# Second feed-forward: gelu twice on ScalarE, four gelu buffers, the convolution taps' wide operations on GpSimd

## What is computed

```python
h = jnp.einsum('bsd,dh->bsh', x, W_exp) + b_exp
h = butterfly(h, up_weights, D_HIDDEN)
h = jax.nn.gelu(h + up_bias, approximate=False)
h = butterfly(h, down_weights, D_HIDDEN)
y = jnp.einsum('bsh,hd->bsd', h, W_con) + b_con
return y + down_bias
```

```python
dt = jnp.exp(log_dt)[:, None]
A = -jnp.exp(log_A_real) + 1j * A_imag
dtA = A * dt
C = (C_real + 1j * C_imag) * (jnp.exp(dtA) - 1.0) / A
vand = jnp.exp(dtA[:, :, None] * t)
K = 2.0 * jnp.einsum('dn,dnl->dl', C, vand).real
```

## Time and profile before

| | us |
|---|---|
| median of 3 runs (2667.52 to 2676.39) | 2668.12 |
| the profiled execution | 2671.26 |
| its span, first to last instruction | 2669.2 |
| TensorE matmuls busy in it | 2289.9 (86%) |
| VectorE busy | 1659.8 (62%) |
| ScalarE busy | 1372.6 (51%) |
| GpSimd busy | 1200.8 (45%) |

### The profile page before, as it was taken

One profiled execution on the slowest core, in us unless ns is written; L12 is line 12 of the kernel. 1 busy time (PEld: TensorE's weight loads), 2 busy tenths in 40 slices (PEclk: granted clock), 3 DMA queues, 4 the chain that ended last, 5 costly groups with the idle time before them and its releaser, 6 DMA issues. The chain is left out here.

```text
span 2669.2 us, 55063 instructions
## 1 busy us (share of the span) xinstructions
PE 2289.9 (86%) x20336; PEld 1601.9 (60%) x20336; DVE 1659.8 (62%) x4170; ACT 1372.6 (51%) x2116; POOL 1200.8 (45%) x1245
## 2 busy tenths in 40 slices
PE   7957777777999888988889987889899879999979
PEld 4535555555666555555555554778566756666658
DVE  6757778776113477767767764666444447777753
ACT  4522222222332288877887885442311457777653
POOL 4329999991001177656756752122365003223220
PEclk9979999998999899999999999999999989999999
DMA  5554445541000111111111111000000100000001
GB/s 179 151 173 135 141 142 153 160 136 63 17 1 28 40 57 56 63 52 57 49 56 53 59 51 42 8 1 1 1 0 1 38 0 1 1 1 1 1 1 64
DMA packets 158733, 149.00 MB, mean 56 GB/s; under 512 B 21441, under 2 KB 141377, under 8 KB 155393
## 3 DMA queue, kind: packets, MB, share of 16 engines
q1 hardware_dynamic: 138704, 105.51, 13.2%
q0 software_dynamic: 3456, 23.07, 2.5%
q10 hardware_dynamic: 16304, 16.83, 2.1%
HBM read 100.51 MB, written 40.63 MB: 53 GB/s over the span
## 5 line engine op out<-in xcount | busy, mean ns | idle before, releaser
L1838 POOL TENSOR_SCALAR a_dist<-a_dist,a_mq 128x512 f32<-128x512 f32 x512 | 357.1, 719 | 120.9 <-ACT a_mq L1777 120.9
L1881 DVE TENSOR_SCALAR_CACHE_REDUCE a_dist<-a_ring 128x512 f32<-128x512 f32 x512 | 332.1, 687 | 90.0 <-PE a_ring L1526 88.6
L1767 ACT ACTIVATE a_pT<-a_psT 128x1024 f32<-128x1024 f32 x256 | 258.3, 1025 | 95.4 <-PE a_psT L1538 87.7
L1538 PE MATMUL a_psT<-ident,a_dist 128*128 128x128 f32 x2048 | 266.3, 277 | 18.0 <-ACT a_pT L1767 17.8
L1538 PEld LDWEIGHTS a_psT<-ident,a_dist 128*128 128x128 f32 x2048 | 235.0, 142 | 50.2 <-issue 20.4
L1761 ACT ACTIVATE a_dist<-a_dist 128x2048 f32<-128x2048 f32 x128 | 236.9, 1902 | 45.1 <-DVE a_dist L1881 42.1
L1526 PE MATMUL a_ring<-a_stack 102*128 102x512 bf16 x512 | 184.2, 398 | 59.1 <-DVE a_dist L1881 35.1
L1526 PEld LDWEIGHTS a_ring<-a_stack 102*128 102x128 bf16 x512 | 47.6, 98 | 230.1 <-DVE a_dist L1881 165.3
L3359 ACT ACTIVATE ds_wtm<-ds_wg,ds_par 128x256 f32<-128x256 f32 x64 | 29.1, 502 | 268.2 <-DVE ds_wg L3489 264.0
L1551 PE MATMUL a_psO<-a_pT,a_va 128*32 128x512 f32 x1024 | 138.0, 616 | 2.3 <-ACT a_pT L1767 2.3
L517 POOL CAST f_h_hi<-f_h 128x512 fp32r<-128x512 f32 x64 | 46.4, 727 | 202.8 <-ACT f_h L506 202.8
(11 more groups left out here) (432 smaller groups left out, 5845.2 us busy)
## 6 DMA issues: line engine op xcount, KB each, us to landing
a_stack<-a_parts_dram SPq DMA_DIRECT2D x384, 64.0 KB
a_parts_dram<-a_parts SPq DMA_DIRECT2D x32, 384.0 KB, 2.5
bf_w<-in_up_w_dram POOLq DMA_DIRECT2D x10, 1024.0 KB
bf_w<-in_down_w_dram POOLq DMA_DIRECT2D x10, 1024.0 KB
ds_nbg<-tok_nbk ACTq DMA_DIRECT2D x128, 64.0 KB
feat_v<-di_part SPq DMA_DIRECT2D x16, 256.0 KB, 2.6
tok_nbk<-di_nbk SPq DMA_DIRECT2D x16, 256.0 KB, 3.0
feat_k<-di_part SPq DMA_DIRECT2D x16, 256.0 KB, 3.4
```

The costliest lines, as they stand in the source:

```text
L1538: last = turn(psT[:, u % 2, kb, q * P:(q + 1) * P], dist[:, g % 2, i, q, k * P:(k + 1) * P], core.ident[:])
L1767: a(pT[:, u // 2, u % 2], psT[:, u % 2], ACT.Exp).then_inc(exp_done, 1)
L1838: last = nc.gpsimd.tensor_scalar(d, d, -1.0, mq[:, g % 2, i, q:q + 1], ALU.mult, ALU.add)
L1881: ts(dist[:, gg % 2, i, q, :], ps[:], 1e-12, 3.0e38, ALU.max, ALU.min, accum_out=mq[:, gg % 2, i, q:q + 1]).then_inc(ring_out, 1)
```

## The change

Four things are edited.

- `h` gets four buffers; the gelu of group n waits for `h_lo` of group n-4.
- ScalarE runs gelu twice on the same PSUM bank: exact into `h`, then into the float32r tensor `h_hi`. GpSimd's copy goes away, and VectorE's subtraction waits for the second gelu. The four normalisations of the next batch come one each after groups 1 to 4.
- The taps' two-input operations on 1024 and 2048 elements, the negation and the eight channel masks go from VectorE to GpSimd (new method `ConvTaps.gpsimd`, 25 steps in one chain with waits for VectorE's and ScalarE's parts). VectorE keeps the 64-wide steps and two roundings. Its pieces move: `between(b, 0)` now stands ahead of a batch's first `h_lo`; the pieces run in (1,0), (1,1), (3,1) and (4,0). ScalarE's two pieces come one batch later.
- `lc_inv`, `lc_w` and `lc_b` are allocated at the other end of SBUF and loaded in `conv_spectra`'s block; their readers wait for them.

The diff, cut to its core:

```diff
+    RING = 4
-        self.h = core.sbuf(f"{tag}_h", [P, 2, S], ctx)
+        self.h = core.sbuf(f"{tag}_h", [P, self.RING, S], ctx)
...
                 act.wait_ge(self.h_ps, n + 1)
-                if n >= 2:
-                    act.wait_ge(self.h_lo_done, n - 1)
-                nc.scalar.activation(self.h[:, m % 2, :], psH[m % 2], ACT.Gelu,
+                if n >= self.RING:
+                    act.wait_ge(self.h_lo_done, n - self.RING + 1)
+                nc.scalar.activation(self.h[:, n % self.RING, :], psH[m % 2], ACT.Gelu, bias=self.bf.bias_h[:, m:m + 1])
+                if m == 0 and b:
+                    act.wait_ge(self.y_ps, TPB * b)
+                nc.scalar.activation(self.h_hi[:, m, :], psH[m % 2], ACT.Gelu,
                                      bias=self.bf.bias_h[:, m:m + 1]).then_inc(self.h_done, 1)
-                if m == NH // 2 and b + 1 < B:
-                    normalize(b + 1)
+                if b + 1 < B and m in (1, 2, 3, 4):
+                    normalize(b + 1, m - 1)
...
-    def gpsimd(self, pool):
-        for n in range(B * self.NH):
-            pool.wait_ge(self.h_done, n + 1)
-            self.nc.gpsimd.tensor_copy(self.h_hi[:, n % self.NH, :], self.h[:, n % 2, :]).then_inc(self.h_hi_done, 1)
...
-        def rest_of_hidden(b, m):
-
-            dve.wait_ge(self.h_hi_done, NH * b + m + 1)
-            tt(self.h_lo[:, m, :], self.h[:, m % 2, :], self.h_hi[:, m, :], ALU.subtract).then_inc(self.h_lo_done, 1)
+        def parts_of_hidden(b, m):
+
+            n = NH * b + m
+            dve.wait_ge(self.h_done, n + 1)
+            tt(self.h_lo[:, m, :], self.h[:, n % self.RING, :], self.h_hi[:, m, :],
+               ALU.subtract).then_inc(self.h_lo_done, 1)
...
         for b in range(B):
+            between(b, 0)
             for m in range(NH):
-                rest_of_hidden(b, m)
-                if m == NH // 2 - 1:
-                    between(b, 0)
+                parts_of_hidden(b, m)
...
         def _(pool):
-            ffn.gpsimd(pool)
+            beside.gpsimd(nc, pool)
...
+    def load_forward(self, sp):
+        sp.dma_start(self.fwd[:], self.sources[0].rearrange("(k p) n -> p k n", p=P)).then_inc(self.fwd_in, 16)
...
-    PHASES, TAPS = 14, 56
+    STEPS, WHOLE, MODES = 6, 8, 31
+    RAW, PHASES, SPREAD, TAPS = 3, 6, 17, 25
...
         if m == 0:
-            pe.wait_ge(self.vec, self.TAPS)
+            pe.wait_ge(self.wide, self.TAPS)
...
-        if n == 2:
-            act.wait_ge(self.vec, self.PHASES)
+        if n == 3:
+            act.wait_ge(self.vec, self.WHOLE)
+            act.wait_ge(self.wide, self.PHASES)
...
-        if n == 3:
+        if n == 4:
...
+        if (n, half) == (1, 1):
+            dve.wait_ge(self.wide, self.RAW)
             step(ts(f[:, 1, :], f[:, 0, :], ROUND, -ROUND, ALU.add, ALU.add))
...
-        if (n, half) == (2, 0):
+        if (n, half) == (3, 1):
             dve.wait_ge(self.act_n, self.ROOTS)
...
-        if (n, half) == (2, 1):
-            cmul_re(T0, NRE, NIM, AR, ABS, RN, FR)
-            cmul_im(T1, NRE, NIM, AR, ABS, RN, FR)
+        if (n, half) == (4, 0):
+            cmul(T0, T1, NRE, NIM, AR, ABS, RN, FR)
...
+    def gpsimd(self, nc, pool):
...
+        def step(ins):
+
+            self.wides += 1
+            ins.then_inc(self.wide, 1)
+            pool.wait_ge(self.wide, self.wides)
+
+        pool.wait_ge(self.loaded, 48)
+        pool.wait_ge(self.vec, self.STEPS)
+        step(tt(f3[0], over_i(TURN), ix, ALU.mult))
+        step(tt(g_im[:], over_j(TURN), jx, ALU.mult))
+        step(tt(self.g_mag, over_j(DR), jx, ALU.mult))
+        pool.wait_ge(self.vec, self.WHOLE)
+        step(tt(f[:, 0, :], f[:, 0, :], f[:, 1, :], ALU.subtract))
+        step(tt(f3[1], over_i(DR), ix, ALU.mult))
+        step(tt(g_im[:], g_im[:], g_re[:], ALU.subtract))
+        assert self.wides == self.PHASES
+        pool.wait_ge(self.act_n, self.ROOTS)
+        step(tt(f[:, 2, :], f[:, 2, :], f[:, 1, :], ALU.mult))
+        step(tt(f[:, 3, :], f[:, 3, :], f[:, 1, :], ALU.mult))
+        pool.wait_ge(self.act_n, self.POWERS)
+        step(tt(g_im[:], g_im[:], self.g_mag, ALU.mult))
+        step(tt(g_re[:], g_re[:], self.g_mag, ALU.mult))
+        pool.wait_ge(self.vec, self.MODES)
+        step(tt(f3[0], over_i(NRE), f3[3], ALU.mult))
+        step(tt(f3[1], over_i(NIM), f3[2], ALU.mult))
+        step(tt(self.f_re[:], f3[0], f3[1], ALU.subtract))
+        step(tt(f3[0], over_i(NRE), f3[2], ALU.mult))
+        step(tt(f3[1], over_i(NIM), f3[3], ALU.mult))
+        step(tt(self.f_im[:], f3[0], f3[1], ALU.add))
+        step(ts(self.f_im[:], self.f_im[:], -1.0, None, ALU.mult))
+        assert self.wides == self.SPREAD
+        for q in range(2):
+            for c in range(CPT):
                 dst = self.fm[:, q].rearrange("p t (i c) -> p t i c", c=CPT)[:, :, :, c]
                 step(ts(dst, (self.f_re, self.f_im)[q][:], self.chan[:, c:c + 1], None, ALU.mult))
...
+        @block.sync
+        def _(sp):
+            lc.load(sp)
+
         @block.tensor
         def _(pe):
-            pe.wait_ge(lc.loaded, 64)
+            pe.wait_ge(lc.fwd_in, 16)
...
+                if i == 0 and u == 0:
+                    pe.wait_ge(lc.loaded, 48)
...
+                            pool.wait_ge(lc.loaded, 48)
```

More of the change, by code:

```diff
@@ L479, in scalar, with normalize @@
         nc, core, psT, psH, NH = self.nc, self.core, self.psT, self.psH, self.NH
-        def normalize(b):
-            if b:
+        def normalize(b, j):
+            if b and j == 0:
                 act.wait_ge(self.tr_done, KD * b)
-            for j in range(TPB):
-                t = TPB * b + j
-                nc.scalar.activation(self.xn[:, j, :], core.X[:, t, :], ACT.Identity, bias=core.shift[:, t:t + 1],
-                                     scale=core.rstd[:, t:t + 1]).then_inc(self.xn_done, 1)
+            t = TPB * b + j
+            nc.scalar.activation(self.xn[:, j, :], core.X[:, t, :], ACT.Identity, bias=core.shift[:, t:t + 1],
+                                 scale=core.rstd[:, t:t + 1]).then_inc(self.xn_done, 1)
         def take_turned(b):
@@ L496, in take_turned @@
                 nc.scalar.activation(self.x_hi[:, k, :], psT[k], ACT.Identity).then_inc(self.x_hi_done, 1)
-        normalize(0)
+        for j in range(TPB):
+            normalize(0, j)
         take_turned(0)
@@ L903, in __init__ @@
         self.vec = core.sem("ck_vec")
+        self.wide = core.sem("ck_wide")
         self.act_n = core.sem("ck_act")
@@ L908, in __init__ @@
         self.steps = 0
+        self.wides = 0
     def allocate(self, core, ctx):
@@ L977, in vector @@
         tt, ts, stt = nc.vector.tensor_tensor, nc.vector.tensor_scalar, nc.vector.scalar_tensor_tensor
-        over_i = lambda t: spread(t, [P, NMT, NI], 2)
-        over_j = lambda t: spread(t, [P, NMT, NJ], 2)
-        f3 = [f[:, q, :].rearrange("p (t i) -> p t i", i=NI) for q in range(4)]
         def step(ins):
@@ L1049, in vector @@
-        if n in (5, 6):
-            q = n - 5
-            for c in range(half * CPT // 2, (half + 1) * CPT // 2):
+            assert self.steps == self.MODES
+    def gpsimd(self, nc, pool):
+        v, idx, f, g_re, g_im = self.v, self.idx, self.f, self.g_re, self.g_im
+        DR, TURN, NRE, NIM = (v[:, q, :] for q in (self.DR, self.TURN, self.NRE, self.NIM))
+        tt, ts = nc.gpsimd.tensor_tensor, nc.gpsimd.tensor_scalar
+        over_i = lambda t: spread(t, [P, NMT, NI], 2)
+        over_j = lambda t: spread(t, [P, NMT, NJ], 2)
+        f3 = [f[:, q, :].rearrange("p (t i) -> p t i", i=NI) for q in range(4)]
+        ix = spread(idx[:, NJ:], [P, NMT, NI], 1)
+        jx = spread(idx[:, 0:NJ], [P, NMT, NJ], 1)
+        def step(ins):
[29 more added lines that the diff above has]
+            for c in range(CPT):
```

54 lines of the change are left out of this document (15 added, 39 removed).

## The result

The changed kernel takes 2663.89 us (median of 20 runs, 2653.31 to 2675.65) beside 2673.73 for the kernel before (20 runs, 2666.5 to 2696.75). The ratio is 0.9957 with a 95% interval of 0.994 to 0.9974: 0.43% less, some 11.5 us, just inside the 0.5% that I called no change. The two medians by themselves differ by 9.8 us. The forecast was 0.5 us less on the same base: right in that it said no change within 0.5%, but a change of some 7 to 16 us, which the interval gives, is clear of the 0.5 us. The profiled execution takes 2666.51 us (span 2664.6).

The account below looks back on a forecast made before the run. TensorE was taken to bound batches 0 and 4 to 7, VectorE's tap work ahead of additions to X to lengthen 1 to 3. Terms +0.6 - 5.5 - 5.7 - 2.9 + 13.6 - 0.3 - 0.3 = -0.5 gave 2667.6 us, range 2646 to 2682.

Parts of the forecast that it names:

- the 60 to 80 that I had set: Sign for batches 1 and 4 together: under 60 us or over 80, the forecast is wrong in the main.
- Gelu twice: ScalarE's second gelu replaces GpSimd's copy: expansion plus 0.6 us per batch, contraction 0.9 less, free batch 24.6.
- Holding: Running GpSimd operations delay VectorE's two-SBUF-input subtractions: one h_lo per GpSimd operation, every 2.75 us (1024) or 5.0 (2048).
- Batch 1: Held h_lo 3.2 us late, roundings before the addition to X 1.2, lower clock 1.5: batch 30.5, -5.5.
- Batch 3: Fifteen small VectorE steps stand ahead of the addition to X, 2.3 us late: batch 26.9, -2.9.
- Batch 4: Subtractions at the pace of GpSimd's run, h_lo 7 11.5 us late, clock 2 to 2.5: batch 38.5, +13.6.
- The masks: Eight strided channel-mask operations on GpSimd, priced at 1.4 us each from its one-input 512-element row.
- The first (no holding): Rival: GpSimd's operations do not hold VectorE; sum -20.0 us, so 2648; chance 15%.
- The second (VectorE starved between operations): Rival: VectorE not served between two GpSimd operations, batch 4's last h_lo 25 us late; +15 to +17, 2684; 8%.
- The third: Rival: GpSimd's wide operations with a broadcast input cost 1.5 times the plain ones; 2687; 5%.
- The fourth: Rival: second gelu costs more than 0.58 us, expansion at 1.9 per group, +21 on top; 2689; 2%.
- The moved loads: Three loads moved from the stage's start to the next block's: cost nothing; uncovered, at most 6.8 us.

Follow-up runs that it names:

- gelu_only: Changed kernel with the taps computed on VectorE as before; second gelu, four buffers, spread normalisation and moved loads kept: stage 216.7 us, ratio to the kernel before 0.9957.
- psum_half: Changed kernel with two of the four gelu buffers in idle PSUM banks instead of SBUF (batches 0 to 6): stage 205.4 us, ratio to the kernel before 0.9897.
- gate: Changed kernel with one more wait: GpSimd's run of six wide operations, negation and masks starts after batch 4's eighth h_lo: stage 206.1 us, ratio 0.9938.
- split4: Changed kernel with each two-input GpSimd operation in four pieces, each waiting for the one before: stage 206.0 us, ratio to the kernel before 0.9930.
- narrow: Changed kernel with each of GpSimd's 25 operations cut to one mode or 16 columns, output incomplete: stage 204.6 us, ratio to the kernel before 0.9920.
- late: Changed kernel with GpSimd's run behind batch 5's h_lo, and nine small VectorE steps heading batch 4, fourteen heading batch 5: stage 218.0 us, ratio 0.9979.
- move: Changed kernel with the fifteen small VectorE steps moved from batch 3's contraction to the head of batch 4: stage 219.0 us, ratio to the kernel before 0.9963.
- gate_move: Changed kernel with GpSimd's run behind batch 4's h_lo and all twenty-three small steps at batch 4's head: stage 210.7 us, ratio to the kernel before 0.9951.
- late_half: Changed kernel with GpSimd's run behind batch 5's h_lo, small steps heading batches 4 and 5, half the gelu buffers in PSUM: stage 217.0 us, ratio 0.9974.

## Why the prediction was right, and where it was not

By its own steps, predicted and measured change of each batch (us): batch 0 +0.6, +0.55; batch 1 -5.5, -9.4; batch 2 -5.7, -5.8; batch 3 -2.9, -1.7; batch 4 +13.6, +9.6; batches 5 and 6 -0.3, -0.36; batch 7 0, 0. Sum -0.5 and -7.5. The direction of each batch held because the mechanism was right: most of the gain of batches 1 to 3 is handed back in batch 4. The total is less well founded. Batches 1 and 4 each came out some 4 us shorter than forecast, batch 3 1.2 longer, and that the sum was still no change within 0.5% owes to the 13 us that this allows. Batches 1 and 4 together are 61.1, inside the 60 to 80 that I had set, near its edge.

**Gelu twice.** Right to the tenth: free batches at 24.5, the contraction at 11.41, the expansion slower by what the bank's cycle says. What I missed is what this part is worth while VectorE is behind. I costed four buffers at nothing and used them only to bound batch 1; the 15.7 us that ScalarE waited for buffers in the trace before did not enter the argument. By gelu_only the feed-forward's edits alone give 6.9 of the 7.5 us. My sentence that some 24 us are the most that the move of the tap work can return was right as a ceiling, but in this kernel the move returns 0.6 of them; with GpSimd's run behind the subtractions it returns 216.7 - 206.1 = 10.6.

**Holding.** Right in kind (psum_half, gate, split4). One subtraction per GpSimd operation: right. VectorE's queue in the changed kernel has the same contrast by itself. In batch 3 the addition of the bias to X has both inputs in SBUF, the addition of `psY` to X has one in PSUM:

```profile
1767.76 4.29 DVE L552 TENSOR_TENSOR X<-X,bf_bias_y 128x256 f32<-128x256 f32 x1
1772.15 0.42 DVE L555 TENSOR_TENSOR X<-f_psY,X 128x256 f32<-128x256 f32 x1
```

GpSimd's powers run beside them, L1063 from 1767.20 to 1771.77 and L1064 from 1771.85 to 1776.53. The first is held for the rest of L1063; the second takes its 0.42 with L1064 under way.

**Batch 1.** The operations with two broadcast inputs are cheaper than the bounds I gave, 1.94 and 3.98 instead of 2.35 (2.1 at the least) and 4.65 (4.2). The small steps ended 1.2 us in and not 3, so h_lo 7 was ready 15.2 us into the batch instead of 18.9. My 15.7 for when it is wanted was too late as well. TensorE reaches h_lo 7 14.1 us into the free batch 2 and 15.2 into batch 1; in batch 4, 22.3:

```profile
1710.98 0.38 PE L459 MATMUL f_psY<-f_down,f_h_hi 128*128 128x256 f32 x1 [0.21 <-DVE f_h_lo L545]
1736.50 0.28 PE L459 MATMUL f_psY<-f_down,f_h_hi 128*128 128x256 f32 x1
1797.29 0.58 PE L459 MATMUL f_psY<-f_down,f_h_hi 128*128 128x256 f32 x1 [0.44 <-DVE f_h_lo L545]
```

So batch 1 lost 1.1 us to late subtractions (3.2 forecast; the 0.21 in the row is only the last of several short gaps), 0.8 before the third tile, to an addition to X that stands behind the roundings (1.2 forecast; in narrow, with the subtractions on time, the roundings cost nothing), and nothing to the clock, granted at 1.00, where I had taken 1.5. That is the -3.9.

**Batch 3.** The fifteen steps take 4.1 us, as said; TensorE waits 1.75 for X (2.3 forecast). The term left out is the clock: 26.34 busy instead of 24.5, at 0.94 over the batch. It is not a fixed price of such a stall, though: psum_half has the same 1.75 at the same place, is granted 1.00 over the batch and loses 0.28.

**Batch 4.** Predicted 24.6 + 11.5 late + 2 to 2.5 behind it for the clock; measured 24.5 + 8.2 late + 1.8. The run began 5.3 us in and not 9.1, since the powers were over 1.5 us in and the small steps ran undelayed; an operation with the subtraction behind it took 2.5 us and not 2.75. h_lo 7 was done 22.2 us in instead of 27.2, and is wanted at 14.1 instead of 15.7. The term for the clock was about right. (The 5.83 idle and 4.18 of longer busy time above are the same 10 us cut another way: between the six stalls TensorE is busy too, at the lower clock.)

**The masks.** Forecast 1.4 us each, measured 3.87: the worst price of the list, from a row of another form. It did no harm in the change, as these hardly hold VectorE and end near 1830, 28 us before TensorE wants them; it is what spoiled late.

**The rivals.** The first (no holding) fell, but the price I gave for its world, -20 us, is what narrow measured, -19.0. The second (VectorE starved between operations) fell with the single subtractions per operation; why the cast of the earlier trace rows was kept waiting for a whole run no run here tests. The third is reversed: broadcast inputs are cheaper, 1.94 beside 2.55 for plain ones of 1024. The fourth fell with the free batches. My evidence against holding, small operations of up to 112 elements that ran free, was no exemption by size: one of 64 elements was held for over 3.2 us in four runs (move, gate_move, late, late_half). The kernel shows what sets those of the earlier trace rows apart: their second input `al` is a PSUM tile (`al = ps("al", [P, 512])`, L3055 of the kernel before). They are the case of psum_half, and I had taken them for operations with two SBUF inputs. One of them, and the GpSimd operation that it meets, in the trace before:

```profile
301.90 0.26 DVE L3435 TENSOR_TENSOR ds_pb<-ds_bg,ds_al 128x88 f32<-128x88 f32 x1
301.65 1.28 POOL L208 TENSOR_TENSOR bf_t<-bf_up,bf_w 128x512 f32<-128x512 f32 x1
```

So the 15% that I gave this rival rested on rows that say nothing for it.

**The moved loads.** Nothing, as said: TensorE is idle for 5.95 us before its first matmul with `lc_inv` after the change, and for 5.91 before it.
